# Ring offsets and landing counts made by VectorE beforehand, loaded by SyncE in the copy loop of a graph transformer layer

## The reference

```python
k, q, v = (_decomp(node_feat, node_type, w_comp_z, w_basis_z) for z in "kqv")   # per node type
kt = einsum('nhi,thij->tnhj', k, relation_att)[edge_type, src]
e  = (q[dst] * kt).sum(-1) * relation_pri[edge_type] * scale
m  = segment_max(e, dst);  ex = exp(e - m[dst]);  a = ex / segment_sum(ex, dst)[dst]
vt = einsum('nhi,thij->tnhj', v, relation_msg)[edge_type, src]
agg = segment_sum(a[..., None] * vt, dst)
out = relu(_decomp(agg, node_type, w_comp_a, w_basis_a) + node_feat @ loop_weight + bias)
return layernorm(x + out)
```

## Time and profile before

| | us |
|---|---|
| runs shown (3) | 1735.99, 1752.89, 1755.89 |
| their median | 1752.89 |
| the profiled execution's own time | 1759.41 |
| its span, first to last instruction | 1757.2 |
| busy: PE, PEld (weight loads) | 1160.7, 962.9 |
| busy: DVE, ACT, POOL | 986.6, 785.6, 881.5 |

### The profile page before, as it was taken

One profiled execution on the slowest core, in us unless ns is written; L12 is line 12 of the kernel. 1 busy time (PEld: TensorE's weight loads), 2 busy tenths in 40 slices (PEclk: granted clock), 3 DMA queues, 4 the chain that ended last, 5 costly groups with the idle time before them and its releaser, 6 DMA issues.

```text
span 1757.2 us, 31429 instructions
## 1 busy us (share of the span) xinstructions
PE 1160.7 (66%) x6730; PEld 962.9 (55%) x6730; DVE 986.6 (56%) x2832; ACT 785.6 (45%) x2217; POOL 881.5 (50%) x915
## 2 busy tenths in 40 slices
PE   8989875657556565566566655566565666656698
PEld 5445434656545554455455554565455565545587
DVE  7877463555445555445555554455554566545677
ACT  4667454444434434443344343443444354434324
POOL 2775354555555554545454545455545554545233
PEclk9999997777677767876777667766777687777699
DMA  8878754555555555545455555555555555555675
GB/s 261 323 289 316 284 172 140 157 148 158 152 159 153 157 151 151 149 141 151 150 163 148 158 152 154 148 160 164 151 162 154 154 168 148 155 150 162 187 242 194
DMA packets 225149, 309.08 MB, mean 176 GB/s; under 512 B 32423, under 2 KB 191119, under 8 KB 217781
## 3 DMA queue, kind: packets, MB, share of 16 engines
q1 hardware_dynamic: 159996, 188.75, 30.6%
q0 software_dynamic: 38880, 106.25, 23.4%
q10 hardware_dynamic: 26088, 12.08, 2.4%
HBM read 139.52 MB, written 58.78 MB: 113 GB/s over the span
## 4 chain that ended last, share of the span: by engine, by line
SPq 34%; issue 31%; PE 12%; DVE 9%; another core or an unknown queue 7%; DMA 2%; DVEq 2%; ACT 1%; POOL 1%; POOLq 0%; ACTq 0%
SPq L1173 27%; PE pb L1900 4%; SPq L1152 2%; PE pb L1923 2%; DVE agg L845 2%; SPq L481 2%; SPq L1170 2%; DVEq L814 2%; DMA kv<-ring 2%; PE pb L2084 1%; SPq L1168 1%; PE pb L2190 1%; PE pb L2028 1%; DVE kv L541 1%
## 5 line engine op out<-in xcount | busy, mean ns | idle before, releaser
L1458 POOL DMA_INDIRECT ring<-table,rows_idx x782 | 745.8, 954 | 736.6 <-SPq L1168 452.5
L2084 PE MATMUL pb<-work,onehot 128*128 128x136 f32 x1664 | 367.5, 358 | 214.1 <-DVE agg L845 152.8
L845 DVE TENSOR_TENSOR agg<-agg,pb 128x136 f32 x832 | 241.8, 291 | 459.9 <-remote 291.8
L2084 PEld LDWEIGHTS pb<-work,onehot 128*128 128x128 f32 x1664 | 307.0, 254 | 242.0 <-issue 210.9
L1650 ACT ACTIVATE work<-pb 128x512 f32<-128x512 f32 x208 | 124.0, 596 | 549.6 <-remote 376.2
L2028 PE MATMUL pb<-q_all,work 128*128 x1664 | 301.0, 340 | 1.3 <-issue 0.8
L2028 PEld LDWEIGHTS pb<-q_all,work 128*128 128x128 f32 x1664 | 280.6, 253 | 7.6 <-issue 4.9
L1637 ACT ACTIVATE work<-lane,neg_lane 128x128 f32<-128x128 f32 x800 | 253.3, 390 | 0.6
L2012 PE MATMUL pb<-ident,onehot 128*128 128x128 f32 x832 | 174.5, 347 | 115.6 <-issue 60.2
L2012 PEld LDWEIGHTS pb<-ident,onehot 128*128 128x128 f32 x832 | 125.4, 180 | 136.0 <-issue 71.3
L686 DVE TENSOR_TENSOR kv<-kv,pb 128x512 f32<-128x512 f32 x208 | 141.5, 680 | 96.6 <-issue 41.7
(11 more groups left out here) (239 smaller groups left out, 1237.2 us busy)
## 6 DMA issues: line engine op xcount, KB each, us to landing
kv<-ring SPq DMA_DIRECT2D x832, 128.0 KB
table<-kv SPq DMA_DIRECT2D x49, 1024.0 KB, 5.2
ring<-table,rows_idx POOLq DMA_INDIRECT x782
kv<-base_rows SPq DMA_DIRECT2D x7, 448.0 KB, 7.6
kv<-in_x_dram SPq DMA_DIRECT2D x8, 384.0 KB, 5.8
seg<-item_bias ACTq DMA_DIRECT2D x48, 64.0 KB
base_rows<-pair ACTq DMA_DIRECT2D x24, 128.0 KB
onehot<-coef_rows SPq DMA_DIRECT2D x3, 1024.0 KB, 5.5
```

The lines of the kernel that those rows point to most:

```text
L845: v.tensor_tensor(a, a, PB[banks[i // 2 % len(banks)]][:, (i % 2) * 256:(i % 2) * 256 + W], ALU.add).then_inc(s_added, 1)
L1458: pool.indirect_dma_start(out=ring[:, o:o + 2 * D], out_offset=None, in_=table, in_offset=bass.IndirectOffsetOnAxis(ap=rows_idx[:, t:t + 1 ...
L2084: mm = t_.matmul(PB[banks[k % len(banks)]][:, u * 256:u * 256 + W], onehot[:, o:o + P], wv[:, b % WR, h * 2 + u, :], start=True, stop=True)
```

## The change

Where VectorE numbers the items, it makes one more number per item: the item's offset in the ring, in elements, that is the tile number (from 0) less 16 times its whole sixteenths, times 256. It takes seven operations on 128x7. The numbers go to HBM as a third row of `item_block` and come back as a row `iplace` on partition 64 of `band`, which grows from 33 to 65 partitions. The counts that wait for the DMAs of the item rows rise from 48 to 64.

SyncE loads the four offsets of a batch, and with a second load the two tile numbers that it waits for. The offset goes into the copy's source as it is.

```diff
-        band = sb("band", [33, 3 * ITEMS // 2])
+        band = sb("band", [65, 3 * ITEMS // 2])
+        iplace = band[64:65, 0:ITEMS].bitcast(i32)
...
                 did(v.tensor_copy(ic[:, 2, :], fc[:, 2, :]))
+                did(v.tensor_scalar(fc[:, 2, :], fc[:, 2, :], -1.0, None, ALU.add))
+                did(v.tensor_copy(ic[:, 3, :], fc[:, 2, :]))
+                did(v.tensor_scalar(ic[:, 3, :], ic[:, 3, :], RING.bit_length() - 1, None,
+                                    ALU.logical_shift_right))
+                did(v.tensor_copy(fc[:, 3, :], ic[:, 3, :]))
+                did(v.scalar_tensor_tensor(fc[:, 2, :], fc[:, 3, :], float(-RING), fc[:, 2, :],
+                                           ALU.mult, ALU.add))
+                did(v.tensor_scalar(fc[:, 2, :], fc[:, 2, :], float(2 * D), None, ALU.mult))
+                did(v.tensor_copy(ic[:, 3, :], fc[:, 2, :]))
...
-            def tiles_of(i, count):
+            def places_of(i, count):
                 return nc.values_load_multi_w_load_instructions(
-                    itile[0:1, i:i + count], engines=(sp.engine,), min_val=1, max_val=REAL,
+                    iplace[0:1, i:i + count], engines=(sp.engine,), min_val=0, max_val=(RING - 1) * 2 * D,
+                    skip_runtime_bounds_check_because="a remainder by the ring's size when written")[1]
+
+            def landings_of(i):
+                return nc.values_load_multi_w_load_instructions(
+                    itile[0:1, i + 1:i + 4:2], engines=(sp.engine,), min_val=1, max_val=REAL,
                     skip_runtime_bounds_check_because="clamped when written")[1]
-            sp.wait_ge(s_item_blocks, 48)
+            sp.wait_ge(s_item_blocks, 64)
...
-                each = tiles_of(4 * n, 4)
+                places = places_of(4 * n, 4)
+                landings = landings_of(4 * n)
                 after(sp, s_weighted, g - 2, NBATCH, b + 1)
...
-                        sp.wait_ge(s_landed, each[u + 1] & 1023)
+                        sp.wait_ge(s_landed, landings[u // 2] & 1023)
                         hold_apart(sp)
                     o = (par * G + b * 4 + u) * 2 * D
-                    sp.dma_start(kv[:, o:o + 2 * D],
-                                 ring[:, bass.ds(((each[u] - 1) & (RING - 1)) * (2 * D), 2 * D)])\
+                    sp.dma_start(kv[:, o:o + 2 * D], ring[:, bass.ds(places[u], 2 * D)])\
                         .then_inc(s_gathered[par][b], 16)
...
-            pool.dma_start(item_block.rearrange("a (p c) -> p a c", c=IPR), ic[:, 1:3, :]).then_inc(s_item_blocks, 16)
+            pool.dma_start(item_block.rearrange("a (p c) -> p a c", c=IPR), ic[:, 1:4, :]).then_inc(s_item_blocks, 16)
             pool.wait_ge(s_item_blocks, 16)
             pool.dma_start(iblk[:, :], item_block[0:1, :]).then_inc(s_item_blocks, 16)
             pool.dma_start(itile[:, :], item_block[1:2, :]).then_inc(s_item_blocks, 16)
+            pool.dma_start(iplace[:, :], item_block[2:3, :]).then_inc(s_item_blocks, 16)
...
-            pe.wait_ge(s_item_blocks, 48)
+            pe.wait_ge(s_item_blocks, 64)
```

More of the change, by code:

```diff
@@ L100, in graph_transformer_layer @@
     coef_rows = nc.dram_tensor("coef_rows", [BLOCKS * NB, P], f32, kind="Internal").ap()
-    item_block = nc.dram_tensor("item_block", [2, ITEMS], i32, kind="Internal").ap()
+    item_block = nc.dram_tensor("item_block", [3, ITEMS], i32, kind="Internal").ap()
     ctx = ExitStack()
@@ L204, in graph_transformer_layer @@
         fc = h1.take(IPR * 6).rearrange("p (k c) -> p k c", k=6)
-        ic = h1.take(IPR * 3).bitcast(i32).rearrange("p (k c) -> p k c", k=3)
+        ic = h1.take(IPR * 4).bitcast(i32).rearrange("p (k c) -> p k c", k=4)
         pad_rows = h1.take(P, PADT).bitcast(i32)
```

## The result

The changed kernel takes 1853.6 us (median of 4 runs, 1843.5 to 1860.3) against 1751.9 us before (4 runs, 1736.0 to 1755.9): a ratio of 1.059, with a 95% interval of 1.051 to 1.068. The forecast was 1691 us with a range up to 1775, so sign and range are both wrong. What happened is the third rival, which stood at 1845 us.

A forecast was written before the change was run, and what follows sets the result against it. SyncE's issuing of copies, slowed beside GpSimd's gathers, was taken to bound the edge stage. The profiled 1759.4 us less 62 of data waits gave 1697; from the median, 6.5 us lower, 1691 us, range 1600 to 1775.

The forecast's parts named there:

- the third rival: Edge stage: SyncE frees slots sooner, GpSimd's gathers join into longer runs, compute stops; 90 us lost, 1845 us, chance 0.12.
- 15 SyncE instructions a batch: SyncE's copy loop: 22 instructions a batch fall to 15, eight ALU operations removed and one load added.
- the pair as one load: SyncE's copy loop: the strided pair of tile numbers was assumed to load as one instruction, 208 more loads in all.
- data waits nearly gone: Edge stage: VectorE's products would hardly wait for copied batches any more, where they had waited 74.4 us.
- SyncE's waits for weighted batches above 50 us: Copy loop: a sign that the forecast is right, SyncE ahead of compute and waiting over 50 us for weighted batches.
- the first-stage edits cost nothing: First stage: VectorE's seven operations cost about 1.2 us or nothing; GpSimd's extra DMA is hidden, the higher count costs nothing.
- the 74.4 us of data waits: Edge stage: VectorE's products waited 74.4 us for copies, the most a faster SyncE could remove; five sixths, 62 us, was forecast.
- three of its own: Signs of being right: GpSimd's "freed" wait below 350 us, added loads at 0.3 to 0.4 us, ScalarE's unnamed waits unchanged.
- the point from which it decides: Gathers join if SyncE's next "freed" comes before four gathers (5.0 us) end; it was put at 5.4 us.
- the counterargument: Against longer gather runs: SyncE may lead by two groups at most, then waits for weighted batches and spaces gathers out.
- its two terms, 167 and 74: Edge stage with gather runs of eight: 167 us more of stopped compute, less 74 us of data waits, 90 us lost.
- A load was taken at 0.34 us: SyncE's copy loop: 208 added loads at the quiet price of 0.34 us, 71 us in all, 200 at the maximum.

## Why the prediction was wrong

What held: 15 SyncE instructions a batch, the pair as one load, data waits nearly gone (17 us), SyncE's waits for weighted batches above 50 us (149), 0.17 us for nearly all of VectorE's new operations, and that the first-stage edits cost nothing (shown by the run with the numbers alone).

The step that failed is the one by which the kernel's gain was bounded: at most the 74.4 us of data waits, "as long as the rest of the compute chain (PE's late signals beside gathers) stays as it is". It did not stay: the unseen waits of VectorE's adds alone rose by 152 us. The prediction had the cause in hand, in its rival 3, and put it at 0.12. Of the signs that it named, rival 3's came (GpSimd's waits for "freed" fewer, 110 for 124, and ScalarE's unnamed waits above 450 us), and three of its own did not: GpSimd waits 550 us for "freed", not below 350, the loads are not at 0.3 to 0.4 us, and ScalarE's unnamed waits are not about as before. Three things kept the rival low.

First, the point from which it decides. The prediction worked out one mean time to the next "freed", 5.4 us against 5.0 for four gathers, and called that "close, but beyond". A mean is no test where the time scatters. Counted in the two traces (runs by the limit of 1.7 us), the next "freed" came within 5.4 us of a run's start in 36% of the runs before and in 48% after. These shares are rough, because beside gathers SyncE's records stand late. In the run of eight shown above its raise is recorded at 889.85, 5.01 us after the start; but GpSimd's sequencer was past its wait ahead of the fifth gather, which needs that raise, at 888.50. In the trace of after, 50 of GpSimd's 383 such waits ended over 1 us before enough raises are on record, in before 36, and with each gather apart none.

Second, the counterargument, that SyncE's lead over compute would space the gathers out. SyncE did run into that wait (149 us in 22 places), but that made a few long pauses (GpSimd's longest wait went from 5.9 to 17.6 us) between runs that stayed long.

Third, the 74.4 us were no price at all. Two runs with the copy loop of before, one of them with the raise moved, had 15 and 32 us of data waits at the same time of 1750 and 1748 us. In the first the unseen waits had grown (765 us for 668), in the second they had not (655). Taking them off a stage in which something else is as late gives nothing.

The price of rival 3 was near: 90 us lost where it is 102, and its two terms, 167 and 74, came out as 152 and 58. That was in part luck, since its count of gathers does not hold. It had runs of 6.3 gathers going to 8; by their starts, at the limit that the breaks showed, there are 137 runs of 5.7 before and 120 of 6.5 after. So 55 more gathers come past the fifth, 69 us at 1.25 us each. The wait also goes on for some 2 us after a run's last gather, and 84 runs have six gathers or more, where 72 had: another 24 us, an estimate from the one run shown.

One term was badly off without deciding anything. A load was taken at 0.34 us. Side by side on SyncE they took 0.79 and 0.63 us in the median, and 121 and 93 us in all 208 batches; less the 63 us of the one load before, that is 151 us more, where the prediction had 71 and a bound of 200. The Trainium skill (DMA: Bandwidth & Descriptors, "Latency and other measured facts") states a floor of about 600 ns for such a load. The changed kernel's medians agree with it; the 0.30 us of the single load before does not. Even so SyncE got ahead: in gather runs it pays by the instruction (in the run shown above one per 0.71 to 0.79 us from 888.34 to 894.32), and it has fewer.

Still open is how gathers hold up TensorE's signals. The records show that a run does it from about its fifth gather on, and that pauses of 1.1 us and more take the loss away, not what is shared. Open too is why a gap of 0.3 us behind every gather gained 150 us and one of 0.64 us behind every fourth nothing.

## What to carry to other kernels

Before an engine is made faster, see whom it releases: where it paces a producer that disturbs everyone else, its slowness may be what keeps the disturbance in pieces, and then the pacing has to be put somewhere on purpose (here 195 operations that compute nothing, worth 8% before the change and 14% after it). A wait whose releaser the profile can't name, on two engines at once and only beside one engine's bursts, is a cause to test first, by breaking the bursts; and a sum of waits is not a bound on a gain where two kinds of wait trade places.

## What the runs showed of the hardware

- In a run of eight gathers at 1.25 us each, three signals of TensorE reached ScalarE and VectorE 6.4 to 7.9 us after their matmuls had ended, together and the oldest last, some 2 us after the last gather. With each gather held apart, some 2.5 us from start to start, no recorded signal for ScalarE's copies was over 0.05 us late.
- A pause of 0.64 us behind every fourth gather did not end this (unseen waits of 976 us, 1860 us in all), one of 1.1 us did in part (562 us, 1606 us), and one of 1.4 us nearly wholly (173 to 241 us, 1592 to 1596 us).
- Beside such runs SyncE's own records stand late, some by over 2 us against GpSimd's, so the order of events between these two engines can't be read there to the microsecond.
- A wait of GpSimd's queue for its own small operation costs far more than the operation: 0.39 us of work behind every gather made some 2.5 us of the 1.25 us between gathers. In that trace the sequencer's load for the next gather starts at 1002.30, after the operation's end at 1002.16; with a break behind every fourth alone, one starts at 1006.08, while a gather runs (1005.63 to 1006.64).
- After TensorE had been busy 0.24 us in 5 us, its granted clock in the next 3.8 us was 0.50, the lower of its two levels (1.2 of 2.4 GHz), as the windows of after show; over the edge stage it was 0.73 after, 0.75 before and 0.78 with the break.
